# Two attention layers in one stream: units interleaved so that a slot's scores and maxima belong to one layer

## The chip, the cores and the metric

The kernel runs on one core of a Trainium2 chip. The metric is the device time of one execution in microseconds (us); lower is better. Three runs of the kernel before gave 1993.62, 1994.18 and 1994.74 us.

Engines are named as the profile does: PE is TensorE (PEld its weight loads), DVE is VectorE, ACT is ScalarE, POOL is GpSimd, SP is SyncE, which here only issues DMAs. PE writes to PSUM, of which this kernel has eight banks in use in the attention stage.

## The reference

Four layers run one after the other on a batch of 8, 256 channels by 512 positions, each added to its input. The change touches only how the first two are ordered against each other:

```python
# layer 0: 16 heads of 16; mask on the keys
Q, K, V = proj(Wq), proj(Wk), proj(Wv)
att = (Q @ K^T / sqrt(16) + b) * m + (1 - m) * NEG
x = x + softmax(att) @ V
# layer 1: 8 heads of 32, keys = queries = values; mask on both sides
qh = x^T @ Wq^T
logits = (qh @ qh^T / sqrt(32) * cmask + (1 - cmask) * NEG) * rmask
x = x + (softmax(logits) @ qh) @ Wo^T
# layer 2: a GRU over 256 steps; layer 3: block attention and layer norm
```

Layer 1 of a batch item needs layer 0 of the same item. Different items do not depend on each other, so layer 1 of one item can run beside layer 0 of the next. The GRU starts when all eight items are done.

## The kernel before

**Units and slots.** The work of one item is cut in six *units* of four heads each: units 0 to 3 are the groups of layer 0, units 4 and 5 those of layer 1 (`UNITS`). A unit has four *slots*, one for each block of 128 keys, so one turn of the loop has 24 slots. In a slot PE does four score matmuls (`ST<-Q,K`, 128 keys by 512 queries, one per head), and ACT takes the exponential of each into `pr`; then the products with the values (`AV<-pr,...`) of the slot before follow, for layer 1 also the sums of the exponentials (`DN<-pr,ones`).

**Maxima.** The softmax needs each query's maximum first. So every unit has, some slots earlier, four slots of *maxima*: PE computes the scores once more, the other way round (`MX<-K,Q`, 128 queries by 512 keys), and DVE reduces each (`mx<-MX`). After the fourth slot of maxima a small transposition (`maxT`, `MX<-identz,mx`) turns them into rows; ACT copies the negated row, POOL splits it in two numbers (`nmp`) and sends both by DMA into two extra rows of the stacked queries, so that the scores come out with the maximum taken off. The scores of a unit wait for this DMA (`nm_dma`).

**Which rows.** Layer 0's stacked operands have 51 (maxima) or 53 rows (scores), and heads lie in pairs at partitions 0 and 64: two such matmuls run side by side on the array. Layer 1's have 97 or 99 rows, and two matmuls run one after the other.

**The order.** A list `ORDER` fixes the order of all these steps, and each engine walks it in order (`Walk`), taking out what is its own. In a slot it is: two scores, two maxima, the value product of the slot before, two scores, two maxima, and then extra steps by a table: projections (`proj`), values, the turning back of a finished unit (`den`, `finish`), `back` and `out`. Maxima stand `LEAD` = 7 slots ahead of their scores. With that lead, slots 0 to 8 of a turn have scores and maxima of layer 0, slots 9 to 15 scores of layer 0 and maxima of layer 1, slot 16 both of layer 1, and slots 17 to 23 scores of layer 1 and maxima of layer 0. Layer 1 runs one item behind layer 0 (`OFF`). The first two turns have a rule of their own (`at_turn`), which takes some maxima eight slots earlier.

**Banks and buffers.** `MX` has three banks in turn, shared by maxima, transpositions and all projections; `ST` has three, so a score waits for the exponential three scores back (`exped`). `AV` and `DN` have one each. Stacked operands of each unit exist once: a unit's stack for the next item is loaded after its last score.

**Stacking.** A projection comes out of PE, ACT and DVE split it in `hi` and `lo`, SP writes both to DRAM (`d_piece`, `pieces`), and reads them back in the stacked layout (`stack`, six or twelve DMAs a unit). Layer 1's queries are masked by POOL in between (`hi_q`, `lo_q`). All this hangs on one SP queue, whose order is written out in the loop at its end. The first maximum of a unit waits for its stack (`stacked`).

Of the kernel before, what the change touches and what calls it, by code (L numbers as in the profile page):

```python
# [5 lines left out]
def attention_layers(nc, xT, K0, ident, to_clear, cleared, preload, preload_late, xt_in, x, mask, wq0, wk0, wv0, b0, wq1, wo1, ident_in):  # L6
# [19 lines left out]
    OFF = [0 if L == 0 else -1 for L, g in UNITS]  # L26
# [6 lines left out]
    with ExitStack() as ctx:  # L33
# [77 lines left out]
        LEAD = 7  # L111

        def at_slot(s):

            w, kc = divmod(s, KC)
            (u, qb, o), = [(u, qb, OFF[u] + (1 if KC * u - LEAD + qb < 0 else 0))
                           for u in range(NU) for qb in range(KC) if (KC * u - LEAD + qb) % SLOTS == s]
            top = [("max", (u, qb, i), o) for i in range(4)]
            pw, pk = divmod((s - 1) % SLOTS, KC)
# [3 lines left out]
            if qb == 0:  # L123

                before = (u - 1) % NU
                t = KC * before - LEAD + KC
                steps.append(("maxT", (before,), OFF[before] + (1 if t < 0 else 0)))
            steps += [st[2], st[3], top[2], top[3]]
            if kc == 1:
                before = (w - 1) % NU  # L130
                o = OFF[before] - (1 if w == 0 else 0)
                if UNITS[before][0] == 1:
                    steps.append(("den", (before,), o))
                steps.append(("finish", (before,), o))
            extra = {1: [("proj", ("q0", 0), 1)], 2: [("proj", ("k0", 0), 1)],
                     3: [("proj", ("q0", 1), 1)], 4: [("proj", ("k0", 1), 1)],
                     6: [("back", (1, 0), -2), ("back", (1, 1), -2)], 7: [("out", (0,), -2)], 8: [("out", (1,), -2)],
                     9: [("values", (1, 0), -1)], 10: [("values", (1, 1), -1)],
                     18: [("back", (0, 0), 0), ("back", (0, 1), 0)],
                     19: [("values", (0, 0), 1)], 20: [("proj", ("k1", 0), 0)], 21: [("proj", ("k1", 1), 0)],  # L140
                     22: [("values", (0, 1), 1)]}
            return steps + extra.get(s, [])

        def at_turn(it, s):
            steps = [(name, a, it + o) for name, a, o in at_slot(s)]
            if it in (0, 1):


                early = lambda step: step[0] in ("max", "maxT") and step[1][0] < 2 and step[2] == 1
                ahead, o = divmod(it * SLOTS + s + 8, SLOTS)  # L150
                own = [step for step in steps if not early(step) and there(step[2])]
                top, turn = ([step for step in ((name, a, ahead + of) for name, a, of in at_slot(o)) if early(step) and step[0] == kind]
                             for kind in ("max", "maxT"))
                steps = []
                for step in own:
                    steps.append(step)
                    if step[0] == "av":
                        steps, turn = steps + turn, []
                    elif step[0] == "score" and step[1][2] % 2 == 1:
                        n = 2 if step[1][2] == 1 else len(top)  # L160
                        steps, top = steps + top[:n], top[n:]
                steps += turn + top
            return steps
        ORDER = [step for it in range(-1, B + 2) for s in range(SLOTS) for step in at_turn(it, s) if there(step[2])]


# [63 lines left out]
        def _(sp):  # L230
# [76 lines left out]
            def first_layer(b):  # L307
                for m in range(2):
                    for side in ("q0", "k0"):
                        pieces(b, side, m)  # L310
# [3 lines left out]
            def second_layer(b, m):  # L314
                for side in ("k1", "q1"):
                    pieces(b, side, m)
                if m == 0:
                    load_in(b + 2)
# [1056 lines left out]
```

## Time and profile before

| | |
|---|---|
| median of three runs | 1994.18 us (1993.62 to 1994.74) |
| profiled execution, time | 1992.88 us |
| profiled execution, span | 1991.1 us |
| PE busy | 1853.8 us, 93% |
| DVE busy | 1144.0 us, 57% |
| ACT busy | 799.3 us, 40% |
| attention stage on PE | first maximum at 33.05 us, last matmul of `out` ends at 947.7 us |

The span is from the first to the last instruction; the time of the execution is 1.8 us longer. The stage that the change touches takes the first 948 us; the rest is the GRU and the last layer, whose instructions do not change. PE's busy time is the union of modelled matmul times, so a PE that looks busy can still be filled badly: what counts is the distance from the start of one slot to the start of the next. A slot starts here with the first of its score matmuls (line 557). Read this way, the five full turns in the middle repeat to within 0.1 us.

### The profile page before, as it was taken

What the parts mean: (1) busy time and instruction counts of PE and PEld (TensorE: products, weight loads), DVE (VectorE), ACT (ScalarE), POOL (GpSimd) and SP (SyncE); (2) the same over time, 40 slices, a digit from 0 to 9 for tenths busy, and PEclk for the clock granted to TensorE, in tenths of its full rate; (3) what the DMA queues carried; (4) which work ended last, traced back from release to release, by engine and by line L of the source; (5) the groups of instructions that cost most, each with busy time, mean ns of one, the idle gap of its engine ahead of it and who ended that gap; (6) DMA issues with size and microseconds to landing.
All of it is one profiled execution on the core that took longest, in us unless ns stands there. A gap on an engine that the chain in (4) does not pass through costs nothing. (4 is left out here: it accounts for less than half of the span.)

```text
span 1991.1 us, 85497 instructions
## 1 busy us (share of the span) xinstructions
PE 1853.8 (93%) x37678; PEld 1269.8 (64%) x37678; DVE 1144.0 (57%) x3363; ACT 799.3 (40%) x2195; POOL 391.5 (20%) x862
## 2 busy tenths in 40 slices
PE   5989999999999999988899999999999999999983
PEld 2434444444444344444899989988888888888861
DVE  4767575766666576723445555555555555555567
ACT  0556565656555565634222222222222222222234
POOL 0121212021211112110131222211222211222113
PEclk7899999999999999988999999999999999999995
DMA  5654433516152534040300000000000000000002
GB/s 146 227 138 141 118 114 87 154 45 185 46 170 65 164 82 124 2 149 1 114 13 13 13 12 13 5 13 13 13 12 11 6 13 12 13 13 10 7 3 85
DMA packets 65521, 127.65 MB, mean 64 GB/s; under 512 B 15545, under 2 KB 22201, under 8 KB 61556
## 3 DMA queue, kind: packets, MB, share of 16 engines
q1 hardware_dynamic: 62076, 121.35, 20.7%
q8 instruction: 296, 4.85, 1.0%
q0 software_dynamic: 3072, 0.82, 0.2%
q14 instruction: 77, 0.63, 0.1%
HBM read 77.56 MB, written 37.85 MB: 58 GB/s over the span
## 5 line engine op out<-in xcount | busy, mean ns | idle before, releaser
L416 DVE TENSOR_REDUCE mx<-MX 128x1 f32<-128x512 f32 x768 | 485.4, 683 | 200.0 <-PE MX L537 199.8
L964 PE MATMUL gate<-whh,state 128*8 128x128 f32 x16384 | 503.6, 273 | 34.0 <-DVE state L880 24.5
L964 PEld LDWEIGHTS gate<-whh,state 128*8 128x8 f32 x16384 | 428.6, 91 | 92.1 <-DVE state L880 86.4
L473 ACT ACTIVATE pr<-ST 128x512 f32<-128x512 f32 x768 | 412.0, 601 | 165.9 <-PE ST L557 165.6
L964 PE MATMUL pg<-whh,state 128*8 128x128 f32 x8192 | 277.1, 273 | 0.3 <-issue 0.3
L857 DVE STREAM_TRANSPOSE trn<-gate 128x128 f32<-128x128 f32 x256 | 81.2, 317 | 337.2 <-PE gate L964 337.2
L912 ACT ACTIVATE rg<-pre 128x32 f32<-128x32 f32 x256 | 58.8, 230 | 505.4 <-DVE pre L859 505.4
L537 PE MATMUL MX<-K,Q 51*128 51x512 f32 (+1 forms) x768 | 246.4, 469 | 14.1 <-DMA Q<-d_rows 9.4
L557 PE MATMUL ST<-Q,K 53*128 53x512 f32 (+1 forms) x768 | 241.0, 486 | 10.5 <-ACT pr L473 10.4
L557 PEld LDWEIGHTS ST<-Q,K 53*128 53x128 f32 (+1 forms) x768 | 99.0, 187 | 207.6 <-ACT pr L473 117.8
L964 PEld LDWEIGHTS pg<-whh,state 128*8 128x8 f32 x8192 | 229.2, 90 | 0.9 <-issue 0.7
L816 POOL TENSOR_TENSOR xT<-xT,state 128x32 f32<-128x32 f32 x256 | 66.9, 261 | 736.3 <-DVE state L880 736.3
L938 PE MATMUL pg<-xT,wih 128*32 128x128 f32 x4096 | 183.0, 275 | 11.5 <-issue 8.7
L537 PEld LDWEIGHTS MX<-K,Q 51*128 51x128 f32 (+1 forms) x768 | 110.0, 194 | 104.1 <-issue 45.1
L361 POOL TENSOR_TENSOR nmp<-nm,zero 16x128 fp32r<-16x128 f32 x48 | 21.5, 447 | 621.5 <-ACT nm L489 621.5
L573 PE MATMUL AV<-pr,va 128*17 128x512 f32 x1024 | 135.6, 601 | 0.9 <-ACT pr L473 0.9
L914 ACT ACTIVATE state<-pre 128x64 f32<-128x64 f32 x256 | 66.7, 261 | 164.6 <-DVE pre L868 164.6
L938 PEld LDWEIGHTS pg<-xT,wih 128*32 128x32 f32 x4096 | 116.0, 110 | 26.2 <-issue 24.8
L880 DVE TENSOR_TENSOR_SCAN state<-by,state 128x48 f32<-128x48 f32 x512 | 104.3, 245 | 41.4 <-ACT by L917 41.4
L948 PE MATMUL gate<-wihZ,xT 128*32 128x128 f32 x2048 | 112.8, 273 | 1.8 <-PEq L33 1.4
L917 ACT ACTIVATE by<-trn 128x16 f32<-128x16 f32 x512 | 90.9, 225 | 22.9 <-DVE trn L871 0.7
L862 DVE STREAM_TRANSPOSE trn<-gate 128x128 f32<-128x128 f32 x256 | 80.9, 316 | 25.2 <-PE gate L964 1.2
(185 smaller groups left out, 1893.5 us busy)
## 6 DMA issues: line engine op xcount, KB each, us to landing
d_q<-hi_q SPq DMA_DIRECT2D x32, 256.0 KB, 3.2
d_q<-lo_q SPq DMA_DIRECT2D x32, 256.0 KB, 3.9
d_k<-hi_k SPq DMA_DIRECT2D x32, 256.0 KB, 3.8
d_k<-lo_k SPq DMA_DIRECT2D x32, 256.0 KB, 3.9
K<-d_k SPq DMA_DIRECT2D x64, 128.0 KB
Q<-d_q SPq DMA_DIRECT2D x64, 128.0 KB
K<-d_k SPq DMA_DIRECT2D x16, 512.0 KB
Q<-d_q SPq DMA_DIRECT2D x16, 512.0 KB
```

The source lines that it names most:

```text
L416: dve.reduce_max(mx[:, u, col:col + 1], bank[:, :], AX.X).then_inc(mx_red, 1)
L473: act.activation(pr[:, kc % 2, i], ST[n % 3][:, :], ACT.Exp, scale=SCALE[UNITS[w][0]]).then_inc(exped, 1)
L537: pe.matmul(bank[:, :], Q[r, h, tok(qb)], K[r, h, :], start=True, stop=True).then_inc(mx_mm, 1)
L557: pe.matmul(ST[n % 3][:, :], K[r, h, tok(kc)], Q[r, h, :], start=True, stop=True).then_inc(st_mm, 1)
L573: last = pe.matmul(AV[r, :], v, pr[:, kc % 2, i, :], start=kc == 0, stop=kc == KC - 1)
L857: dve.transpose(trn[:, R, :], psR[:, 0:P]).then_inc(s_tr, 1)
L862: dve.transpose(trn[:, N, :], psN[:, 0:P]).then_inc(s_tr, 1)
L880: dve.tensor_tensor_scan(state[:, 1 - q, W3 * a:W3 * a + W3], by[:, half(a)].rearrange("p c b v -> p (c b v)"), threes(q, a), 0.0, ALU.mul ...
L917: a.activation(by[:, half(z), :, 2], tr[Z][:, half(z)], ACT.Sigmoid).then_inc(s_z[z], 1)
L938: last = pe.matmul(gb[i % 2][32 * j:32 * j + 32, 0:TG * B], wih[:, n, i * P + 32 * j:i * P + 32 * j + 32], xT[:, n, TG * blk:TG * (blk + 1 ...
L948: last = pe.matmul(zb[32 * j:32 * j + 32, P * w:P * (w + 1)], xT[:, k, t0:t0 + 4, :].rearrange("p t b -> p (t b)"), wihZ[:, k, P * w:P * ( ...
L964: last = pe.matmul(bank[32 * j:32 * j + B, lo:hi], held[q][:, c, :], whh[:, c, o + lo:o + hi], start=first, stop=done)
```

## The change

The order of the six units in a turn becomes a list, `PLACES` = (0, 1, 5, 2, 3, 4): scores go through the units in this order, four slots each. Maxima are taken for the unit three places later: beside scores of 0, 1, 5, 2, 3, 4 stand maxima of 2, 3, 4, 0, 1, 5. Unit 5 now runs two items behind layer 0, unit 4 one. The extra steps move to other slots, `at_turn` loses its rule for the first turns, and the loop has one turn more at its end. SP's order follows. No instruction of PE, ACT, DVE or POOL is added or removed, and the same DMAs are issued.

```diff
-    OFF = [0 if L == 0 else -1 for L, g in UNITS]
+    OFF = [0 if L == 0 else -1 - g for L, g in UNITS]
...
-        LEAD = 7
+        PLACES = (0, 1, 5, 2, 3, 4)
+        LEAD = len(PLACES) // 2
...
-            w, kc = divmod(s, KC)
-            (u, qb, o), = [(u, qb, OFF[u] + (1 if KC * u - LEAD + qb < 0 else 0))
-                           for u in range(NU) for qb in range(KC) if (KC * u - LEAD + qb) % SLOTS == s]
+            p, kc = divmod(s, KC)
+            w = PLACES[p]
+
+            def maxima(p):
+                u = PLACES[(p + LEAD) % NU]
+                return u, OFF[u] + (1 if p + LEAD >= NU else 0)
...
-            extra = {1: [("proj", ("q0", 0), 1)], 2: [("proj", ("k0", 0), 1)],
...
-                     19: [("values", (0, 0), 1)], 20: [("proj", ("k1", 0), 0)], 21: [("proj", ("k1", 1), 0)],
...
+            extra = {0: [("proj", ("k1", 0), -1)], 2: [("proj", ("q0", 0), 1)], 3: [("proj", ("k0", 0), 1)],
+                     4: [("proj", ("k1", 1), -1)], 5: [("proj", ("q0", 1), 1)], 7: [("proj", ("k0", 1), 1)],
+                     14: [("back", (1, 0), -2), ("back", (1, 1), -2)], 15: [("out", (0,), -2)], 16: [("out", (1,), -2)],
+                     17: [("values", (1, 0), -1)], 18: [("values", (1, 1), -1)],
+                     21: [("values", (0, 0), 1)], 22: [("back", (0, 0), 0), ("back", (0, 1), 0)], 23: [("values", (0, 1), 1)]}
...
-        ORDER = [step for it in range(-1, B + 2) for s in range(SLOTS) for step in at_turn(it, s) if there(step[2])]
+        ORDER = [step for it in range(-1, B + 3) for s in range(SLOTS) for step in at_turn(it, s) if there(step[2])]
...
-            for it in range(-1, B):
+            for it in range(-1, B + 1):
+                layer(it - 1, ("k1", "q1"), 0)
+                place(it - 1, LAST0 + 1)
+                layer(it + 1, ("q0", "k0"), 0)
+                place(it + 1, 0)
+                layer(it - 1, ("k1", "q1"), 1)
...
+                place(it + 1, 1)
+                place(it - 1, LAST1)
+                place(it + 1, 2)
+                place(it + 1, LAST0)
+                load_in(it + 2)
```

Three places on PE show it. In the rows `ST` and `MX` are PSUM banks of scores and maxima, `K0,Q0` are the stacks of layer 0, `K1,Q1` those of layer 1. Line numbers of the change are 17 lower.

**In a full turn**, a slot with scores of layer 1. Before, PE had:

```order
L557 MATMUL ST1<-Q1,K1 128x512
L557 MATMUL ST2<-Q1,K1 128x512
L537 MATMUL MX2<-K0,Q0 128x512
L537 MATMUL MX0<-K0,Q0 128x512
L573 MATMUL AV<-pr,vb 32x512 x4
L576 MATMUL DN<-pr,ones 32x512 x4
L557 MATMUL ST0<-Q1,K1 128x512
L557 MATMUL ST1<-Q1,K1 128x512
L537 MATMUL MX1<-K0,Q0 128x512
L537 MATMUL MX2<-K0,Q0 128x512
```

Now such a slot reads:

```order
L540 MATMUL ST0<-Q1,K1 128x512
L540 MATMUL ST1<-Q1,K1 128x512
L520 MATMUL MX2<-K1,Q1 128x512
L520 MATMUL MX0<-K1,Q1 128x512
L556 MATMUL AV<-pr,vb 32x512 x4
L559 MATMUL DN<-pr,ones 32x512 x4
L540 MATMUL ST2<-Q1,K1 128x512
L540 MATMUL ST0<-Q1,K1 128x512
L520 MATMUL MX1<-K1,Q1 128x512
L520 MATMUL MX2<-K1,Q1 128x512
```

The scores and the products are the same; the maxima between them were of layer 0 and are of layer 1. The maxima of layer 0 now stand only in slots whose scores are of layer 0.

**At the end of the attention stage**, where the last item's layer 1 begins. Before, PE had, after the last value products of item 6, its turning back and its output projection, and then the first maxima of item 7:

```order
L573 MATMUL AV<-pr,vb 32x512 x4
L576 MATMUL DN<-pr,ones 32x512 x4
L557 MATMUL ST0<-Q1,K1 128x512
L557 MATMUL ST1<-Q1,K1 128x512
L573 MATMUL AV<-pr,vb 32x512 x4
L576 MATMUL DN<-pr,ones 32x512 x4
L583 MATMUL MX1<-sel,rawd 128x4 x4
L591 MATMUL MX2<-identz,raw 128x128 x4
L630 MATMUL MX0<-identz,yT1 128x128 x4
L630 MATMUL MX1<-identz,yT1 128x128 x4
L638 MATMUL MX2<-w1,ctxs 128x256 x4
L638 MATMUL MX0<-w1,ctxs 128x256 x4
```

Now the two projections of item 7 (`w1`) come directly ahead of the scores and maxima that use them:

```order
L556 MATMUL AV<-pr,vb 32x512 x4
L559 MATMUL DN<-pr,ones 32x512 x4
L527 MATMUL MX2<-identz,mx 16x128
L587 MATMUL MX0<-x1,w1 128x512 x2
L566 MATMUL MX1<-sel,rawd 128x4 x4
L574 MATMUL MX2<-identz,raw 128x128 x4
L587 MATMUL MX0<-x1,w1 128x512 x2
L540 MATMUL ST1<-Q1,K1 128x512
L540 MATMUL ST2<-Q1,K1 128x512
L520 MATMUL MX1<-K1,Q1 128x512
L520 MATMUL MX2<-K1,Q1 128x512
L540 MATMUL ST0<-Q1,K1 128x512
```

Of these, the two rows on `K1,Q1` into `ST` are scores of item 6, and the rows into `MX` at the end are the first maxima of item 7, unit 4, for which the first projection in this piece is needed. The turning back and output of item 6 moved behind them.

**Ahead of the last unit's scores.** Before, the transposition of the last unit's maxima is followed by the scores of unit 4 and their products:

```order
L544 MATMUL MX0<-identz,mx 16x128
L557 MATMUL ST2<-Q1,K1 128x512
L557 MATMUL ST0<-Q1,K1 128x512
L557 MATMUL ST1<-Q1,K1 128x512
L557 MATMUL ST2<-Q1,K1 128x512
L573 MATMUL AV<-pr,vb 32x512 x4
L576 MATMUL DN<-pr,ones 32x512 x4
L557 MATMUL ST0<-Q1,K1 128x512
L557 MATMUL ST1<-Q1,K1 128x512
L557 MATMUL ST2<-Q1,K1 128x512
L557 MATMUL ST0<-Q1,K1 128x512
L573 MATMUL AV<-pr,vb 32x512 x4
```

Now it stands after all scores of unit 4, and the last unit's scores follow it after one turning back (`sel`, `raw`):

```order
L556 MATMUL AV<-pr,vb 32x512 x4
L559 MATMUL DN<-pr,ones 32x512 x4
L527 MATMUL MX0<-identz,mx 16x128
L566 MATMUL MX1<-sel,rawd 128x4 x4
L574 MATMUL MX2<-identz,raw 128x128 x4
L540 MATMUL ST0<-Q1,K1 128x512
L540 MATMUL ST1<-Q1,K1 128x512
L540 MATMUL ST2<-Q1,K1 128x512
```

The distance between the last maxima and the scores that need them shrank to the two steps between.

## Rows read from the trace of the kernel before

**Rows 1.** Stretches: us, busy of PE, PEld, DVE, ACT, POOL, PEclk, DMA share, GB/s.

```profile
449.49:559.23 109.74, 107.06 (x591) 47.40 (x588) 71.81 (x118) 63.16 (x123) 19.66 (x29) 1.00 0.39 112
449.49:490.95 41.46, 39.27 (x214) 16.73 (x211) 28.98 (x47) 25.54 (x50) 3.96 (x8) 1.00 0.66 187
```

**Rows 2.** Timeline, scores and maxima of layer 0, no extra step (start us, us).

```profile
792.22 0.51 PE L557 MATMUL ST<-Q,K 53*128 53x512 f32 x2
...
792.76 2.06 ACT L473 ACTIVATE pr<-ST 128x512 f32<-128x512 f32 x4 [0.86 <-PE ST L557]
...
795.14 0.50 PE L557 MATMUL ST<-Q,K 53*128 53x512 f32 x2
```

**Rows 3.** Timeline, PE: the same kind of slot, just after one with an extra step.

```profile
152.94 0.49 PE L557 MATMUL ST<-Q,K 53*128 53x512 f32 x2
...
155.22 0.40 PE L557 MATMUL ST<-Q,K 53*128 53x512 f32 x1
```

**Rows 4.** Timeline, PE: scores of layer 0, maxima of layer 1.

```profile
392.40 0.49 PE L557 MATMUL ST<-Q,K 53*128 53x512 f32 x2
...
395.64 0.50 PE L557 MATMUL ST<-Q,K 53*128 53x512 f32 x2
```

**Rows 5.** Timeline, PE: scores of layer 1, maxima of layer 0.

```profile
335.73 0.82 PE L557 MATMUL ST<-Q,K 99*128 99x512 f32 x2
...
336.92 1.07 PE L573 MATMUL AV<-pr,vb 128*32 128x512 f32 x8
337.80 1.04 PE L576 MATMUL DN<-pr,ones 128*32 128x512 f32 x8
...
339.77 0.69 PE L557 MATMUL ST<-Q,K 53*128 53x512 f32 x2
```

**Rows 6.** Timeline, PE: scores and maxima of layer 1, value products of layer 0.

```profile
297.44 0.68 PE L557 MATMUL ST<-Q,K 99*128 99x512 f32 x2
...
300.61 0.40 PE L557 MATMUL ST<-Q,K 99*128 99x512 f32 x1
```

**Rows 7.** Timeline, PE: from slot to slot over a projection, layer 0's, then layer 1's.

```profile
465.21 0.51 PE L557 MATMUL ST<-Q,K 53*128 53x512 f32 x2
...
469.85 0.50 PE L557 MATMUL ST<-Q,K 53*128 53x512 f32 x2
...
536.19 0.82 PE L557 MATMUL ST<-Q,K 99*128 99x512 f32 x2
...
541.75 1.03 PE L557 MATMUL ST<-Q,K 99*128 99x512 f32 x2
```

**Rows 8.** Timeline, PE: scores of layer 1 with no maxima beside them.

```profile
916.02 0.96 PE L557 MATMUL ST<-Q,K 99*128 99x512 f32 x3
...
919.55 0.96 PE L557 MATMUL ST<-Q,K 99*128 99x512 f32 x3
```

**Rows 9.** Timeline, DVE: maxima with no scores beside them.

```profile
33.88 7.26 DVE L416 TENSOR_REDUCE mx<-MX 128x1 f32<-128x512 f32 x12 [8.86 <-PE MX L537]
```

**Rows 10.** Timeline, last item: layer 1's first projection, unit 4's stack, unit 5's.

```profile
856.08 1.88 PE L604 MATMUL MX<-x,w 128*128 128x512 f32 x4
...
865.96 1.14 SPq L286 DMA_DIRECT2D K<-d_k  x2
...
878.49 1.14 SPq L286 DMA_DIRECT2D K<-d_k  x2
```

**Rows 11.** Timeline, the last unit's row of maxima: transposition, DMA.

```profile
912.18 0.38 PE L544 MATMUL MX<-identz,mx 128*16 128x128 f32 x2
...
913.88 1.00 POOL L372 DMA_DIRECT2D Q<-nmp  x2
```

**Rows 12.** The page, DMA issues: KB each, median us to landing.

```profile
Q<-nmp POOLq DMA_DIRECT2D x96, 8.0 KB, 2.1
```

**Rows 13.** Timeline, PE: the output projection of item 6, and of item 7.

```profile
879.81 6.71 PE L638 MATMUL MX<-w,ctxs 128*128 128x256 f32 x16 [0.68 <-ACT ctxs L515]
...
943.99 3.72 PE L638 MATMUL MX<-w,ctxs 128*128 128x256 f32 x16 [0.73 <-ACT ctxs L515]
```

More of the change, by code:

```diff
@@ L109, in half_of @@
             return w // 2 if w <= LAST0 else w - LAST0 - 1
-        LEAD = 7
+        PLACES = (0, 1, 5, 2, 3, 4)
+        LEAD = len(PLACES) // 2
         def at_slot(s):
-            w, kc = divmod(s, KC)
-            (u, qb, o), = [(u, qb, OFF[u] + (1 if KC * u - LEAD + qb < 0 else 0))
-                           for u in range(NU) for qb in range(KC) if (KC * u - LEAD + qb) % SLOTS == s]
-            top = [("max", (u, qb, i), o) for i in range(4)]
-            pw, pk = divmod((s - 1) % SLOTS, KC)
+            p, kc = divmod(s, KC)
[3 more added lines that the diff above has]
+                return u, OFF[u] + (1 if p + LEAD >= NU else 0)
+            u, o = maxima(p)
+            top = [("max", (u, kc, i), o) for i in range(4)]
+            earlier = (s - 1) % SLOTS
+            pw, pk = PLACES[earlier // KC], earlier % KC
             st = [("score", (w, kc, i), OFF[w]) for i in range(4)]
             steps = [st[0], st[1], top[0], top[1], ("av", (pw, pk), OFF[pw] - (1 if s == 0 else 0))]
[L123 to L127, printed above, removed]
+            if kc == 0:
+                u, o = maxima((p - 1) % NU)
+                steps.append(("maxT", (u,), o - (1 if p == 0 else 0)))
             steps += [st[2], st[3], top[2], top[3]]
             if kc == 1:
-                before = (w - 1) % NU
-                o = OFF[before] - (1 if w == 0 else 0)
+                before = PLACES[p - 1]
+                o = OFF[before] - (1 if p == 0 else 0)
                 if UNITS[before][0] == 1:
@@ L142, in at_slot @@
             return steps + extra.get(s, [])
         def at_turn(it, s):
[L145 to L162, printed above, removed]
@@ L163, in at_turn @@
-            return steps
-        ORDER = [step for it in range(-1, B + 2) for s in range(SLOTS) for step in at_turn(it, s) if there(step[2])]
+            return [(name, a, it + o) for name, a, o in at_slot(s)]
+        ORDER = [step for it in range(-1, B + 3) for s in range(SLOTS) for step in at_turn(it, s) if there(step[2])]
         number = {}
@@ L305, in stack, with layer, place @@
                     put(Q1[3 * n:3 * n + 1, of, :], d_rows[b:b + 1, 4:5, :].to_broadcast([1, 4, T]))
-            def first_layer(b):
-                for m in range(2):
-                    for side in ("q0", "k0"):
+            def layer(b, sides, m):
+                if there(b):
+                    for side in sides:
                         pieces(b, side, m)
-                    for w in units_of(0, m):
-                        stack(b, w)
[L314 to L318, printed above, removed]
-                for w in units_of(1, m):
-                    stack(b, w)
-            for it in range(-1, B):
+            def place(b, w):
+                if there(b):
+                    stack(b, w)
+            for it in range(-1, B + 1):
[4 more added lines that the diff above has]
+                layer(it - 1, ("k1", "q1"), 1)
                 if there(it):
```

15 lines of the change are left out of this document (2 added, 13 removed).

## The prediction, made before the changed kernel ran

> **What bounds the kernel now.** I read the page first: the span and PE's share (93%). Then busy time by stretch: in a full turn of 109.74 us PE is busy 107.06, DVE 71.81, ACT 63.16, and DMA is a share of 0.39 [rows 1]. So in the middle of the attention stage PE bounds, and what a turn costs is the sum of its slots' lengths on PE. I then read the timeline of PE, from the first score matmul of a slot to that of the next, for each kind of slot. The reader is to see that the kinds differ although the matmuls are alike:
>
> - Both of layer 0: 2.92 us, with ACT idle 0.86 us before its four exponentials, which take 2.06 [rows 2]. Here PE is not the bound: the second pair of scores waits for its banks. After a slot with an extra step the same work takes 2.28 us [rows 3]. PE's own need is thus about 2.28, and 0.65 is a wait that other work can fill.
> - Scores of layer 0, maxima of layer 1: 3.24 [rows 4]; over several such slots 3.2.
> - Scores of layer 1, maxima of layer 0, with `DN`: 4.04 [rows 5]. `DN` is 0.88 of it: the `AV` products start at 336.92 and `DN` at 337.80, for the same work.
> - Both of layer 1: seen only beside `AV` of layer 0, 3.17 [rows 6]. With `DN` I take 3.17 + 0.88 = 4.05. This is the main kind that the trace doesn't show. From above it is bounded by the mixed slot's 4.04, if sorting is worth nothing; from below by 3.9, if half of the 0.24 to 0.3 us between two pairs of unlike shape goes. I keep 4.05, the sum of rows, as the value, and 3.9 as the low end.
>
> Last I read the end of the stage, for what the last item waits for.
>
> **The steady part, counted.** The order gives how many slots of each kind there are in all. Before: 78 with both of layer 0, 49 mixed with scores of layer 0, 42 mixed with scores of layer 1, 8 with both of layer 1 and no `DN`, 14 with scores of layer 1 alone, 1 with scores of layer 0 alone, 15 with maxima alone. Now: 120, 0, 0, 15, 4, 8, 12, and 45 with both of layer 1 and `DN`. Scores of layer 1 alone take 3.53 [rows 8]; of layer 0 alone no row shows; ACT's 2.06 is the lower bound, 2.92 with maxima the upper, and 3.53 less `DN`, 2.65, is what I take. Maxima alone are 7.26 us for 12, so 2.42 for four [rows 9].
>
> For both of layer 0 the bounds are 2.28 and 2.92. The nine such slots at the start of a turn last 41.46 us [rows 1]; their extra steps I put at 16.7 (four projections 7.6, two output products 3.8 by rows 13, one `DN` 0.9, and by estimate 4.4 for turning back and `maxT`). That leaves 2.75 each, and I take that.
>
> Before: 78 x 2.75 + 49 x 3.2 + 42 x 4.04 + 8 x 3.17 + 14 x 3.53 + 2.65 + 15 x 2.42 = 654.8. Now: 120 x 2.75 + 15 x 3.17 + 45 x 4.05 + 4 x 3.53 + 8 x 2.65 + 12 x 2.42 = 624.2. The difference is **-30.6 us**; with 2.92 it is -23.5, with 2.28 it is -50.3. All of it comes from slots of layer 0: a mixed pair costs 7.24, a sorted one 6.80.
>
> **What the moved steps give back.** Layer 1's projections stood in slots with scores of layer 1 and cost 541.75 - 536.19 - 4.04 = 1.52 each; in slots of layer 0 a projection costs 4.64 - 2.75 = 1.89 [rows 7], because a bank of `MX` is then held until ACT and DVE have both read it. 16 x 0.37 = +5.9. `DN` of a unit's last slot falls into a slot of layer 0 twelve times instead of six: 6 x 0.88 = +5.3. Layer 1's values, now in slots of layer 0: +1. Together **+12**. `back` and `values` of layer 0 stay in slots of layer 1: nothing. The SP queue: each stack now has eight slots (over 30 us) between its last reader and its first maximum, where it had thirteen. From the start of a layer 1 projection to the end of its stack I find 18 us (below), so nothing waits in a full turn; POOL's rows have eight slots where they had three.
>
> A rule that speaks for more than this: the Trainium skill, TensorEngine Tiling (Array Packing), section Key Properties, says that changing the tiling mode drains TensorE. A mixed pair has ten such changes, a sorted pair four. The rows bear it out only where PE is the bound: (7.24 - 2.28 - 4.05) / 6 = 0.15 us a change. By the rule the gain of the slots would be -50.3, not -30.6; it is the first rival.
>
> **The ends.** Here the change loses, since layer 1 of the last item is spread over more of the order.
>
> - *Waiting for the last stack.* Before, layer 1's first projection for the last item starts at 856.08, its stack's first DMA is issued at 865.96, and the second unit's stack, which waits for pieces queued behind the first stack, at 878.49 [rows 10]. The first stack is then in place between 869.5 (all issued) and 878; I take 874.5, 18.4 us after the projection's start. Before, PE had the scores of unit 5 and the whole turning back and output of item 6 to do meanwhile. Now, by the order, after this projection come only `den`, `finish`, the second projection and two scores, 6 us. **+12.5 us** (8 to 16).
> - *After it* PE restarts at half clock. What this costs can be seen on the output products: 6.71 us for item 6, after waits of PE, and 3.72 for item 7 [rows 13]. +3 for the first slots after the wait, and -3 because item 6's output now follows busy work: 0.
> - *Three more ends of a run of scores,* where the products wait for the last exponential, less one that goes: +2.4.
> - *The last row.* From the transposition to the end of POOL's issue are 2.70 us [rows 11], to landing some 2 more [rows 12]. Before, fourteen score matmuls stood between; now `den` and `finish`, about 2 us. +2.8.
> - *The start:* four more maxima before the first score and none of the eight-slots-early rule, +1.5. In the second turn four slots have maxima of layer 1 alone, at the risk of half clock after: +1.5 (0 to 3).
>
> Together **+20.7**.
>
> **The sum.** -30.6 + 12.2 + 20.7 = +2.3 us. Walking through the new order stretch by stretch instead, with the same slot lengths, I get +1.6 up to the second turn, -9 over that turn, 5 x -2.3 over the full turns, +3 in the turn that has no new item, and +24 from there to the end: +8. The two differ in how much of the waits the extra steps fill. I take the middle, **+5**: the profiled execution of 1992.88 would be 1998, and on the median of 1994.18, which lies 1.3 above it, **1999 us**. A full turn should be 107.4 us, 2.3 less, and the attention stage end near 953.
>
> **Rivals.**
>
> 1. *The drains are what costs, everywhere.* Extra steps fill all waits in slots of layer 0, which come down to 2.28, halfway 2.5. For it: rows 3. Against it: the nine slots of [rows 1] have extra steps in seven and still average 2.75. Full turn 104 to 106; time by the sum -50.3 + 12.2 + 20.7 = -17, halfway -8: 1977 to 1987, say **1986**. This is the one that ends on the other side, faster; it decides if the average of slots of layer 0 falls below 2.6.
> 2. *Slots of layer 0 get longer, not shorter.* Sixteen in place of nine, six projections in them in place of four, three banks of `MX` for all: the average stays at 2.92 and each extra step costs in full. For it: DVE idles in projection slots while the bank waits for ACT. -23.5 + 12.2 + 25 = +14: **2008**.
> 3. *The end costs nothing.* The last stack arrives early, since x1 and the other stacks are not in its way: the wait is 5 instead of 12.5, with the sum as it is otherwise: **1992**, no change.
> 4. That the change doesn't do what it says: the order shows that it does. A deadlock or a late stack in the full turns would need 30 us of DMA where 18 are seen; less than 1 in 50.
>
> **Chances.** The forecast 0.55 (own range 1992 to 2005), rival 1 0.23, rival 2 0.12, rival 3 0.10. The range that leaves out 2 in 10 is 1983 to 2009. A difference of 0.2% is 4 us, about what a measurement tells from none. Faster by more: 0.23 of rival 1 and a little of the others, 0.27. Within: rival 3 and the lower third of the forecast's range, 0.31. Slower: 0.42.
>
> **What would show it.** In the changed profile: slots with both of layer 1 at 4.05 and 3.17; slots of layer 0 at 2.75 on average over a turn; a full turn from one xin load to the next at 107.4; a wait of PE of some 12 us for a stack, near the end, ended by a DMA into `K1` or `Q1`, with half clock after it. The forecast is wrong if a full turn is under 106 or over 109, or if that wait is under 8 or over 17 us.

## The result: faster by 0.47%

| | before | changed |
|---|---|---|
| median of 9 runs each, same chip | 1994.74 us (1990.89 to 2005.3) | 1985.56 us (1975.8 to 1994.08) |
| profiled execution, time and span | 1992.88, 1991.1 us | 1987.19, 1985.4 us |
| first matmul of the GRU | 949.1 us | 945.6 us |

The ratio is 0.9953, with a 95% interval of 0.9935 to 0.9971. 1999 us was forecast; rival 1 had said 1986. The changed kernel was run once more beside before (e8 below), with 0.9962 (0.9946 to 0.9977).

The attention stage of both, by stretch: to the second turn, the second turn, five full turns, the rest up to the GRU. Columns as in [rows 1]. Before:

```profile
0.00:127.16 127.16, 100.08 (x396) 43.83 (x396) 74.58 (x128) 46.34 (x88) 19.62 (x37) 0.84 0.54 162
127.16:230.04 102.88, 99.30 (x531) 42.07 (x531) 64.92 (x108) 60.48 (x117) 20.78 (x28) 1.00 0.47 132
230.04:778.65 548.61, 535.23 (x2942) 236.93 (x2940) 359.20 (x590) 315.76 (x611) 98.27 (x145) 1.00 0.40 115
778.65:949.10 170.45, 155.92 (x840) 75.68 (x837) 79.95 (x130) 83.67 (x163) 21.42 (x33) 0.91 0.20 60
```

The changed kernel:

```profile
0.00:123.72 123.72, 94.47 (x389) 41.00 (x390) 73.42 (x126) 44.21 (x86) 17.53 (x35) 0.85 0.60 164
123.72:223.26 99.54, 97.02 (x444) 41.06 (x444) 67.17 (x112) 50.48 (x99) 18.03 (x26) 0.85 0.44 123
223.26:751.02 527.76, 512.71 (x2941) 235.03 (x2940) 358.53 (x590) 310.43 (x610) 99.20 (x145) 1.00 0.42 116
751.02:945.64 194.62, 166.95 (x935) 80.99 (x935) 78.49 (x128) 92.82 (x182) 26.35 (x38) 0.91 0.23 71
```

-3.4, -3.3, -20.9 and +24.2 make -3.5 us. The rest of the span's 5.7 is a GRU and last layer whose instructions did not change: their part is 1041.9 us before, 1039.8 after. Over the fourteen profiles of this study this part took between 1037.1 and 1043.3 us with the same instructions, so 2 us there say nothing on the order. Of the 9.2 us between the medians the profiles thus show 3.5 as the attention stage's own (3.7 in the second pair, e8 and e11). Both profiled executions of the changed kernel were slower than their medians (1987.19 against 1985.56, 1988.34 against 1983.84); where the rest of the 9.2 comes from is not shown.

A full turn here is one pass of the loop with work of every kind in it. Within one, PE is busy 102.52 of 105.53 us, where it was 107.06 of 109.74 [rows 1]:

```profile
434.27:539.80 105.53, 102.52 (x589) 47.00 (x589) 71.70 (x118) 62.09 (x122) 19.85 (x29) 1.00 0.42 116
```

The timeline of PE in that turn, a plain slot of layer 0 behind a projection, which answers to [rows 3]; it lasts 2.23 us:

```profile
463.67 0.50 PE L540 MATMUL ST<-Q,K 53*128 53x512 f32 x2
464.01 0.40 PE L520 MATMUL MX<-K,Q 51*128 51x512 f32 x2
464.33 1.05 PE L556 MATMUL AV<-pr,va 128*17 128x512 f32 x8
465.32 0.49 PE L540 MATMUL ST<-Q,K 53*128 53x512 f32 x2
465.65 0.75 PE L520 MATMUL MX<-K,Q 51*128 51x512 f32 x2
465.90 1.09 PE L540 MATMUL ST<-Q,K 53*128 53x512 f32 x2
```

A slot of layer 0 with one half of an output, 4.24 us (499.46 to 503.70), and PE waits for nothing in it:

```profile
499.46 0.50 PE L540 MATMUL ST<-Q,K 53*128 53x512 f32 x2
...
501.77 1.99 PE L621 MATMUL MX<-w,ctxs 128*128 128x256 f32 x8
503.70 0.50 PE L540 MATMUL ST<-Q,K 53*128 53x512 f32 x2
```

And the new kind, both of layer 1 with `DN`, which no row of before could show: 4.27 us, from 478.64 to 482.91; its neighbour takes 4.12.

```profile
478.64 0.70 PE L540 MATMUL ST<-Q,K 99*128 99x512 f32 x2
479.18 0.91 PE L520 MATMUL MX<-K,Q 97*128 97x512 f32 x2
480.02 1.06 PE L556 MATMUL AV<-pr,vb 128*32 128x512 f32 x8
480.90 1.04 PE L559 MATMUL DN<-pr,ones 128*32 128x512 f32 x8
481.88 0.73 PE L540 MATMUL ST<-Q,K 99*128 99x512 f32 x2
482.44 0.63 PE L520 MATMUL MX<-K,Q 97*128 97x512 f32 x2
482.91 0.40 PE L540 MATMUL ST<-Q,K 99*128 99x512 f32 x1
```

In the second turn, where four slots have maxima of layer 1 alone, the clock falls to 1.2 GHz at about 164 us and comes back near 195:

```profile
160.00:170.00 10.00, 9.38 (x26) 4.32 (x25) 9.72 (x18) 0.97 (x2) 1.94 (x4) 0.71 0.89 208
170.00:180.00 10.00, 10.00 (x37) 3.88 (x37) 5.72 (x10) 4.57 (x11) 1.89 (x4) 0.50 0.36 97
180.00:190.00 10.00, 10.00 (x37) 3.48 (x34) 5.13 (x9) 5.37 (x12) 0.77 (x2) 0.50 0.32 79
190.00:200.00 10.00, 9.96 (x55) 4.86 (x54) 6.78 (x12) 5.54 (x12) 1.26 (x3) 0.76 0.05 8
```

DVE is busy 9.72 of the first ten us and takes one maximum at a time. PE waits for it, and then runs the next slots of layer 0 at half the clock while busy throughout. Near the end stand the three waits the prediction spoke of, in the timeline of PE; the first one is for the last item's stack, the second for the last row of maxima, and the third row is the last output, now partly at half clock [rows 10, 11, 13]:

```profile
848.28 1.04 PE L540 MATMUL ST<-Q,K 99*128 99x512 f32 x2
861.33 1.22 PE L520 MATMUL MX<-K,Q 97*128 97x512 f32 x2 [12.01 <-DMA Q<-d_rows]
...
912.63 0.63 PE L574 MATMUL MX<-identz,raw 128*128 128x128 f32 x4
915.02 3.25 PE L540 MATMUL ST<-Q,K 99*128 99x512 f32 x6 [1.76 <-DMA Q<-nmp]
...
938.70 5.51 PE L621 MATMUL MX<-w,ctxs 128*128 128x256 f32 x16 [0.67 <-ACT ctxs L498]
```

### The profile page after: what moved, and what is told of

Its sections match the earlier page's. It is cut to its first block and busy times, and to the rows that moved or that the text cites. A ratio compares the mean times of both kernels' runs of the same rounds, so it can differ in the third digit from the quotient of the medians.

```text
span 1985.4 us, 85497 instructions
## 1 busy us (share of the span) xinstructions
PE 1830.9 (92%) x37678; PEld 1268.2 (64%) x37678; DVE 1143.2 (58%) x3363; ACT 789.8 (40%) x2195; POOL 392.4 (20%) x862
## 5 line engine op out<-in xcount | busy, mean ns | idle before, releaser
L520 PE MATMUL MX<-K,Q 51*128 51x512 f32 (+1 forms) x768 | 238.7, 444 | 25.3 <-DMA Q<-d_rows 22.5
L921 PE MATMUL pg<-xT,wih 128*32 128x128 f32 x4096 | 173.6, 274 | 7.7 <-issue 6.7
L520 PEld LDWEIGHTS MX<-K,Q 51*128 51x128 f32 (+1 forms) x768 | 121.6, 196 | 78.5 <-DVE mx L399 38.8
L931 PE MATMUL gate<-wihZ,xT 128*32 128x128 f32 x2048 | 108.0, 273 | 1.4 <-PEq L33 1.4
```

The source lines that it names most:

```text
L520: pe.matmul(bank[:, :], Q[r, h, tok(qb)], K[r, h, :], start=True, stop=True).then_inc(mx_mm, 1)
L921: last = pe.matmul(gb[i % 2][32 * j:32 * j + 32, 0:TG * B], wih[:, n, i * P + 32 * j:i * P + 32 * j + 32], xT[:, n, TG * blk:TG * (blk + 1 ...
L931: last = pe.matmul(zb[32 * j:32 * j + 32, P * w:P * (w + 1)], xT[:, k, t0:t0 + 4, :].rearrange("p t b -> p (t b)"), wihZ[:, k, P * w:P * ( ...
```

## The experiments

All but e4 and e11 are timed against before on their own chip; ratios carry 95% intervals.

**e1: the places kept, the sorting undone.** With maxima two places ahead instead of three, sixteen of the 24 slots are mixed again.

```diff
-        LEAD = len(PLACES) // 2
+        LEAD = 2
```

> The change with maxima two places ahead instead of three, and nothing else altered: scores still go 0, 1, 5, 2, 3, 4 and every extra step keeps its slot, but per turn 8 slots have both of layer 0, 8 mix scores of layer 0 with maxima of layer 1, and 8 mix scores of layer 1 with maxima of layer 0; none has both of layer 1. Theory A (sorting the shapes on PE is the gain): a sorted pair costs 2.62 + 4.05 = 6.7 us, a mixed pair 7.2, so a full turn goes from 105.6 to about 109.7, and the whole is 25 to 30 us slower than the change, slower than the kernel before. Theory B (the gain comes from where the extra steps stand, which fill waits in slots of layer 0): a full turn stays within 1 us of 105.6, and the time within 5 us of the change.

Measured: ratio 1.0301 (1.0276 to 1.0325), 2049.36 us against 1990.43. The full turn:

```profile
467.55:577.72 110.17, 108.58 (x590) 47.62 (x590) 72.08 (x118) 62.41 (x122) 19.81 (x29) 1.00 0.39 111
```

That is 4.6 us more than the changed kernel's, and 0.4 more than before's. Slot by slot the eight left sorted repeat to 0.02 us, the eight with scores of layer 0 and maxima of layer 1 add 3.6 us (0.45 each on average, 0.07 to 0.83 in single slots), the eight the other way round 1.06 (0.13 each). A mixed pair (one slot of each kind) thus costs 0.58 us more than a sorted one; the prediction had 0.44. Before has seven mixed pairs a turn and e1 eight, so of the 0.43 us between them the eighth pair is 0.58, and all the moved steps together are about -0.15. At 0.58 a pair, sorting is 4.1 of the 4.2 us that a turn gained, and moving the steps cost nothing. This takes the average of e1's pairs for those of before, which stand beside other steps.

Theory A gave 25 to 30 us for the whole and was far too low: e1's GRU starts 58.5 us later than the changed kernel's. 23 of these are the five full turns. The other 35 come from its ends: 24 before the second turn (148.08 us instead of 123.72), where only eight slots of the first turn have scores and maxima side by side, instead of sixteen, and 11 behind the last full turn.

**e4: what a change of shape costs by itself.** Between attention and GRU PE runs six sequences of matmuls that wait for nothing: *small* ones (51 rows, in pairs), *large* ones (97 rows) and *cols* (the eight rows of an `AV` of one slot).

```diff
+            for n in range(12):
+                small(0), small(1), small(0), small(1), large(0), large(1), large(0), large(1)
...
+            for n in range(24):
+                small(0), small(1), large(0), large(1)
...
+            for n in range(48):
+                small(0), small(1)
...
+            for n in range(48):
+                large(0), large(1)
...
+            for n in range(12):
+                cols()
+                small(0), small(1), small(0), small(1)
...
+            for n in range(12):
+                cols()
+                large(0), large(1), large(0), large(1)
```

> The change with extra matmuls on PE between the attention stage and the GRU, which nothing reads and which wait for nothing but each other: pairs of 51 rows (two side by side) and pairs of 97 rows, in runs of like pairs, in alternation, and each beside column-tiled value products. The whole is longer by their length. Theory A (a change of shape on the array costs PE time of its own): pairs in alternation take longer than the mean of two runs of like pairs, by 0.15 us for each change of shape. Theory B (no such cost; mixed slots are longer for waits on ACT and DVE): alternation costs less than 0.03 us a change.

The six stretches, in the order of the diff (one profile, not timed):

```profile
943.52:965.01 21.49, 21.48 (x97) 11.68 (x97) 0.00 (x0) 0.00 (x0) 0.00 (x0) 1.00 0.00 1
965.99:992.09 26.10, 26.10 (x100) 11.61 (x97) 0.00 (x0) 0.00 (x0) 0.00 (x0) 1.00 0.00 1
993.07:1004.20 11.13, 11.13 (x100) 8.95 (x97) 0.00 (x0) 0.00 (x0) 0.00 (x0) 1.00 0.01 1
1005.18:1027.17 21.99, 21.99 (x101) 17.96 (x97) 0.00 (x0) 0.00 (x0) 0.00 (x0) 1.00 0.00 0
1029.01:1048.76 19.75, 19.75 (x148) 5.16 (x144) 0.00 (x0) 0.00 (x0) 0.00 (x0) 1.00 0.01 2
1048.76:1070.96 22.20, 22.20 (x129) 8.73 (x125) 0.00 (x0) 0.00 (x0) 0.00 (x0) 1.00 0.00 0
```

A stretch runs from the first start of its kind to the start of the next sequence, so each holds one change at its end. 96 small matmuls then take 11.13 - 0.2 = 10.93 us, 0.114 each, and 96 large ones 21.79, 0.227 each. The first sequence has 48 of each, 16.36 us, and 24 changes: (21.49 - 16.36) / 24 = 0.21 a change. The second has the same matmuls and 48 changes: 9.74 / 48 = 0.20. One `cols` is 0.86 us (two in a row before a small one last 1.84, one 0.98). The fifth stretch has twelve groups of four small ones, twelve `cols` and 24 changes: (19.75 - 15.78) / 24 = 0.17; the sixth eleven groups of large ones, ten `cols` and 21 changes: (22.20 - 18.59) / 21 = 0.17. A change thus has a price of its own, the same after two matmuls as after four. The Trainium skill, TensorEngine Tiling (Array Packing), Key Properties, says that changing the tiling mode drains TensorE, with no figure; the trace agrees that a change takes time, 0.17 to 0.21 us, though it can't show that the time is a drain.

With these numbers half of e1 can be accounted for. A mixed slot has three more changes than a sorted one: 0.60 us. Scores of layer 1 with small maxima instead of large: 0.60 - 4 x 0.113 = +0.15, measured +0.13. Scores of layer 0 with large maxima: 0.60 + 0.45 = +1.05, measured +0.45. Part of the missing 0.60 is waits that the sorted slot still has and the mixed one fills: over these eight slots PE idles 1.97 us in a full turn of the changed kernel (0.72 for exponentials, the rest for maxima on DVE and for ACT's copy of them) and 0.43 in e1, 0.19 a slot. The other 0.4 a slot stays open.

**e5: the extra steps bunched.** Turning back and both output halves stand in slot 14, both values steps in slot 17; slots 15, 16 and 18 lose theirs.

```diff
-                     14: [("back", (1, 0), -2), ("back", (1, 1), -2)], 15: [("out", (0,), -2)], 16: [("out", (1,), -2)],
-                     17: [("values", (1, 0), -1)], 18: [("values", (1, 1), -1)],
+                     14: [("back", (1, 0), -2), ("back", (1, 1), -2), ("out", (0,), -2), ("out", (1,), -2)],
+                     17: [("values", (1, 0), -1), ("values", (1, 1), -1)],
```

> The change as it is, but the steps that stand alone in the layer 0 slots 14, 15, 16 (turning back, output, output) stand together in slot 14, and both values steps in slot 17: slots 15, 16 and 18 lose their step. Nothing else moves. Theory A (an extra step costs less than its own time, since it fills the wait for the exponentials of its slot): slots 15, 16 and 18 rise by 0.4 to 0.65 us over what they have less their step, slot 14 takes the two output halves at their full 1.9 us each, and a full turn goes from 105.55 to 106.8 to 107.5; five full turns +6 to +10. Theory B (a step costs its own time wherever it stands; slots of layer 0 are short in the changed kernel for another reason): a full turn stays within 0.3 us of 105.55.

Measured: ratio 1.0033 (1.0011 to 1.0054). The full turn, the same work:

```profile
429.48:536.66 107.18, 102.75 (x589) 47.44 (x588) 71.45 (x118) 61.97 (x122) 19.86 (x29) 1.00 0.42 114
```

107.2 against 105.5: the same steps cost 1.65 us more a turn in two heaps, so theory B is out, and the total is theory A's. Its slots are not. Set against their length in the changed kernel without their step, slots 15 and 18 are 0.1 us shorter and slot 16 is 0.2 longer, where 0.4 to 0.65 was expected of all three. The wait for exponentials is back only one slot behind the first plain one: 0.22 and 0.25 us in slots 16 and 17, and slot 19 is 0.54 longer. The other part is in the two heaps, each 0.56 us longer than its slot and its steps were apart. In slot 14 it is the output, which now waits for ACT's copy of what was turned back, a wait that another slot's work covered in the changed kernel:

```profile
494.09 0.63 PE L613 MATMUL MX<-identz,yT 128*128 128x128 f32 x4 [0.28 <-DVE mx L399]
495.39 3.72 PE L621 MATMUL MX<-w,ctxs 128*128 128x256 f32 x16 [0.67 <-ACT ctxs L498]
```

So spread steps do cost less than bunched ones, for two kinds of wait: that for exponentials, and that of one step for the step ahead of it.

**e2: a new order at the end.** The scores of item 6's unit 5 stand between the projections of item 7 and its first maxima, where before had them; turning back and output of item 6 lie beside the maxima.

```diff
+        for k in range(KC):
+            ORDER += end_slot(score=(5, k, six), av=(5, k - 1, six) if k else None)
+        ORDER += end_slot(av=(5, 3, six), extra=[("den", (5,), six), ("finish", (5,), six)])
+        ORDER += [("back", (1, 0), six), ("back", (1, 1), six)]
+        ORDER += end_slot(top=(4, 0, seven))
+        ORDER += end_slot(top=(4, 1, seven), extra=[("out", (0,), six)])
...
```

> The change with the order after the last turn rewritten: the scores of unit 5 of item 6 come before the wait for the last item's stack, without maxima between them; den, finish and back of item 6 too; out and values stand among the maxima of unit 4 of item 7, and two slots of maxima of unit 5 stand ahead of the scores of unit 4. Theory A (the end's wait of 12.0 us for the stack, the cold slots behind it and the wait for the last row are a cost of the new order that another order avoids): the attention stage ends 12 to 14 us earlier than with the change, at about 931 us, and the time falls as much, to about 1973. Theory B (the wait is only moved, since the work put into it was hiding the reduction of the maxima): it ends less than 4 us earlier.

Measured: 0.9945 (0.9924 to 0.9966), 1978.17 us against 1990.43; the GRU starts at 937.1 us, 8.5 earlier. Theory A had 12 to 14 us and a start at 931, theory B less than 4: neither. The wait of 12.01 us is gone, so it did cost; not all of it came back. From the start of item 7's turn the stage takes 187.3 us instead of 194.6, so 7.4 are the new end's and 1.2 come from a shorter head. Part of what is missing is half clock in the work behind. PE in its timeline, with the waits just before and at the fall of the clock, at 865.6 us (0.78 granted over 860 to 870 us):

```profile
860.91 1.06 PE L585 MATMUL AV<-pr,vb 128*32 128x512 f32 x8 [0.94 <-ACT pr L485]
...
864.02 1.05 PE L595 MATMUL MX<-sel,rawd 128*128 128x4 f32 x8 [1.19 <-ACT rawd L495]
...
866.42 1.97 PE L642 MATMUL MX<-identz,yT 128*128 128x128 f32 x8 [0.85 <-DVE yT L452]
```

**e7: the same with maxima begun earlier,** beside the last scores of item 6, and unit 5's beside scores of unit 4.

```diff
-            ORDER += end_slot(score=(5, k, six), av=(5, k - 1, six) if k else None)
+            ORDER += end_slot(score=(5, k, six), top=(4, 0, seven) if k == 3 else None, av=(5, k - 1, six) if k else None)
...
+        ORDER += end_slot(score=(4, 0, seven), top=(5, 1, seven))
+        ORDER += end_slot(score=(4, 1, seven), top=(5, 2, seven), av=(4, 0, seven))
+        ORDER += end_slot(score=(4, 2, seven), top=(5, 3, seven), av=(4, 1, seven))
```

> The tail order again, with the first maxima of item 7's unit 4 started beside the last scores of item 6's unit 5 and all maxima of unit 5 but the first four beside scores of unit 4. Theory A (what is left at the end is that maxima and scores stand apart, 1.9 us a pair of slots, and the half clock from 865 to 897 us after the gaps around turning back): the GRU starts 4 to 8 us earlier than in the tail order (937.1), at 929 to 933. Theory B (the last item's chain of DMAs, transposition and exponentials sets the end, whatever PE does meanwhile): 935 to 938.

Measured: 0.9922 (0.9899 to 0.9945), GRU at 932.0, inside theory A's 929 to 933. But 1.8 of the 5.1 us lie ahead of item 7's turn: from the start of item 7's turn to the GRU it takes 184.0 us, in e2 187.3, in the changed kernel 194.6. The end itself is 3.3 shorter, where theory A had 4 to 8.

**e3: the second turn's lone maxima moved** beside the scores of slots 12 to 15.

```diff
+                if 12 <= s <= 15:
+                    at = [n for n, step in enumerate(steps) if step[0] == "max" and step[1][2] in (1, 3)]
+                    for n, half in zip(reversed(at), ((2, 3), (0, 1))):
+                        steps[n + 1:n + 1] = [("max", (LAST0 + 1, s - 12, i), 0) for i in half]
```

> The change with the four slots of the second turn that hold only maxima (unit 4, item 0) dissolved: these maxima stand beside the scores of unit 2 in the next four slots, where layer 0's maxima already are. Theory A (that run of maxima alone lets the granted clock of PE fall, and the nine slots behind it run at 4.6 to 5.0 us instead of 2.9): the clock stays at 1.00 from 157 to 200 us; the four slots take 5.0 to 5.3 us by DVE, and the third turn starts 6 to 10 us earlier than at 223.3 us. Theory B (the clock falls all the same, since DVE is the bound in the doubled slots): it starts less than 3 us earlier, or later.

Measured: 0.9997 (0.9979 to 1.0015), third turn at 222.22 us instead of 223.26. Theory B, and a miss for the repair: eight maxima a slot keep DVE the bound, the clock falls at the same place, and slots 13 to 15 take 7.3 us each.

**e6: the same maxima spread thinner,** two behind each of slots 7 and 12 to 18.

```diff
+                if s in (7, *range(12, 19)):
+                    n = 0 if s == 7 else s - 11
+                    steps += [("max", (LAST0 + 1, n // 2, 2 * (n % 2) + i), 0) for i in range(2)]
```

> The change, but in the second turn the sixteen maxima of unit 4, item 0, that stood alone in slots 8 to 11 are spread two a slot behind slots 7 and 12 to 18. Theory A (PE falls to half clock because it waits for DVE in a stretch of maxima; with six maxima a slot DVE needs 6 x 0.6 = 3.6 us and PE some 2.8): the granted clock stays 1.00 from 157 to 200 us and the third turn starts at 214 to 219 instead of 223.3. Theory B (the fall at 165 us has nothing to do with the maxima that stand alone, as the run in which they were moved beside slots 12 to 15 hints: it fell at the same time): half clock again from 165 to some 190, third turn at 222 to 226.

Measured: 0.9956 (0.9938 to 0.9973), third turn at 218.0. The clock still falls at 162 us, but is back at 173. Neither theory as stated; in e9, with the same second turn, the third began at 221.3. So this order doesn't settle the cause.

**e10: the lone maxima computed twice.** Sixteen matmuls more, nothing moved.

```diff
+                if b == 0 and u == LAST0 + 1:
+                    pe.matmul(bank[:, :], Q[r, h, tok(qb)], K[r, h, :], start=True, stop=True)
                 pe.matmul(bank[:, :], Q[r, h, tok(qb)], K[r, h, :], start=True, stop=True).then_inc(mx_mm, 1)
```

> The change, with each of the sixteen maxima matmuls of unit 4, item 0, issued twice into the same bank: 3.7 us more work for PE in slots 8 to 11 of the second turn, where it waits for DVE otherwise (2.4 us a slot). Theory A (half clock comes from PE's waits for DVE in these slots): the fall at 165 us is gone or short, slots 13 to 17 are back at 2.9, 2.9, 2.9, 3.1 and 4.3, third turn at 214 to 217. Theory B (half clock comes from something else): it falls at the same place, and the third turn starts at 223 or up to 4 us later.

Measured: 0.9946 (0.993 to 0.9962), 1977.91 us against 1988.79. Its third turn starts at 216.68, 6.6 us earlier than in the changed kernel's first profile, with more work on PE:

```profile
160.00:170.00 10.00, 10.00 (x46) 5.24 (x38) 9.69 (x18) 0.83 (x3) 2.01 (x4) 1.00 0.90 213
170.00:180.00 10.00, 9.53 (x44) 3.54 (x43) 7.77 (x13) 6.78 (x14) 1.89 (x4) 0.83 0.51 124
180.00:190.00 10.00, 9.27 (x62) 4.40 (x62) 8.17 (x15) 6.72 (x15) 2.04 (x4) 1.00 0.33 85
190.00:200.00 10.00, 9.98 (x62) 4.63 (x58) 7.25 (x12) 8.04 (x17) 1.06 (x3) 1.00 0.24 64
```

DVE is as busy as in the changed kernel in the first stretch and sets the pace, but PE has no gaps and keeps 2.4 GHz there; only 3.4 us near 173 are at half. One profile would not do, since the spell changes from execution to execution. Six profiles (the changed kernel twice, e2, e4, e5, e7) have the same instructions up to slot 13 of the second turn: in them the spell lasts 10.2 to 30.7 us and the turn takes 92.6 to 99.5. In the two profiles with doubled maxima (this one and e12) it lasts 3.4 us and not at all, and the turn takes 92.0 and 90.7. The shortest of the six is e5's:

```profile
160.00:170.00 10.00, 9.44 (x26) 4.61 (x25) 9.28 (x18) 1.83 (x5) 1.54 (x5) 0.64 0.94 208
170.00:180.00 10.00, 9.57 (x50) 3.18 (x48) 7.54 (x13) 6.10 (x13) 1.04 (x3) 0.84 0.23 66
```

So filling PE's short waits for DVE keeps the clock up for most or all of the stretch, and theory A holds for the clock; how much time that gives lies between 0.6 and 8.8 us by which profiles are compared. The timed ratios do not tell e10 (0.9946) from the change (0.9953 and 0.9962). The Trainium skill, TensorE: Matmul & The Clock Gate, A second HAM failure mode: psum-queue depth-cycling, tells of a kernel in which short idle times between groups of matmuls, as PSUM banks go round, let the clock go up and down; the trace agrees, with PE busy 9.38 of 10 us where the clock falls in the changed kernel and 10.00 of 10 here.

**e9 and e12: parts together.** e9 has e6's spread maxima and e7's end with two repairs: the first maxima one slot later, and `den` and `finish` of unit 4 ahead of the last unit's scores. e12 has e10's doubled maxima and e9's end.

```diff
+        ORDER += end_slot(top=(4, 0, seven))
...
+        ORDER += end_slot(av=(4, 3, seven), extra=[("den", (4,), seven), ("finish", (4,), seven)])
+        ORDER += end_slot(score=(5, 0, seven))
```

> Both repairs in one kernel: the spread maxima of unit 4 in the second turn, and the new order at the end, there with the first maxima of item 7 one slot later (after the scores of item 6's last unit) and with den and finish of unit 4 put between the last row's transposition and the scores that need it. Theory A (the parts add): the third turn starts some 4 to 5 us earlier than in the changed kernel, the end is another 13 to 16 us shorter than there (13.7 with the first new order; the two waits of 2.53 and 2.86 us mostly go), so the GRU starts at 924 to 930, against 945.7, and the median is 1964 to 1972. Theory B (the waits at the end move to other places and the cold start stays): GRU start 931 to 937, median 1973 to 1980.

> The doubled maxima of the run before, in place of the spread ones, together with the new order at the end of the run that had both. Theory A (the second turn's half clock and the end are separate costs and add): third turn at 213 to 216, GRU start at 923 to 928, median 9 to 14 us under that of the run with spread maxima and the new end when both are set against before: a ratio of 0.988 to 0.992. Theory B (a shorter start makes the end colder or its transfers later, as between the tail orders): GRU start 929 to 932 and a ratio of 0.993 to 0.995.

Measured for e9: 0.9945 (0.9931 to 0.9958), GRU at 930.6. The two waits that it was to remove went, from 2.53 to 0.27 us and from 2.86 to none, and from the start of item 7's turn to the GRU it is 181.6 us; but its third turn starts only 2 us earlier than the changed kernel's, and the median and GRU start are theory B's (1973 to 1980, 931), not theory A's 1964 to 1972. For e12: **0.9882 (0.9867 to 0.9896), 1965.4 us against 1987.63.** Its third turn starts at 215.88 us and its GRU at 926.5:

```profile
926.55 3.70 PE L960 MATMUL gate<-wihZ,xT 128*32 128x128 f32 x128 [1.44 <-PEq L33]
```

Theory A held: the two repairs add. e9 and e12 differ only in how they treat the second turn's maxima, spread or doubled, and their ratios (0.9945 and 0.9882) lie clear of each other. This is the best kernel of the study, 22 us under before where the change alone brings 9.

**e8 and e11: both kernels once more.**

> The changed kernel once more, unchanged, beside the kernel before on the same chip. If the 8.6 us between the medians is the change's: a ratio of 0.994 to 0.998, attention end 943 to 947 in its profile, full turns 105.5. If part of it was the spread of the unchanged GRU stage: a ratio nearer 1, with the attention stage some 3 to 6 us shorter than 949.1 as in the first profile.

> The kernel before, unchanged, for a second profile. If the attention stage of before repeats from execution to execution (no half clock after 65 us but at the last item): GRU start within 1 us of 949.1, full turns 109.7. If it has spells of its own: a difference of several us, which would put part of the measured gain down to chance.

e8: 0.9962 (0.9946 to 0.9977), full turns of 105.6 us, GRU at 945.7. e11, one profile: full turns of 109.7, GRU at 949.4, 0.3 from the first. So before's attention stage repeats, and the gain is the change's, though the profiles show less of it (3.5 and 3.7 us) than the medians (9.2 and 8.9).

## Why the prediction was wrong

- **What failed is the steady part, in two terms.** A full turn was to be 107.4 us and is 105.5. The sorted pair was set at 0.44 us less than a mixed one (7.24 and 6.80); it is 0.58 less (e1), 1.0 us over a turn's seven pairs. And the moved steps were set at **+12** in all, 5.9 of it because a projection costs "1.89" in a slot of layer 0 and 5.3 for `DN` in such slots; by e1 they cost about nothing (-0.15 a turn), the other 0.9 us of the turn.
- **In slots, it is the "2.75" for a slot of layer 0.** The eight slots of layer 1 in a full turn sum to 37.6 us, so the sixteen of layer 0 are 67.9. With each step's own time on PE taken off (25.8 us in all) that is 2.64 a slot. The nine slots of before, reckoned alike, have 2.78. The sixteen are not fuller: eleven have a step from the table, where before seven of nine had. But the steps are of other kinds. The eight slots with the projections keep 2.69, the eight with turning back, output and values 2.58. The new kind, both of layer 1 with `DN`, erred the other way: 4.12 and 4.27 for the 4.05 that was set, and the low end of 3.9 did not come.
- **Why the steps cost less is shown in part.** Slots 1 to 7 take 30.4 us with four projections and 23.5 in the turn that has none of these four: 1.74 each, not 1.89. In the kernel before the same four, in slots 1 to 4, cost 2.00 each (25.07 us against 17.06 over slots 1 to 5). e5 shows that spreading other steps is worth 1.65 us a turn. Which of these waits made up the whole 0.9 us was not taken apart.
- **Rival 1 is nearest to what came.** It had a turn of 104 to 106 and 1986 us; 105.5 and 1985.6 were measured. But it was to decide "if the average of slots of layer 0 falls below 2.6", and 2.64 is just over. Its strong form, 2.28 and all of the drains, did not come: a pair's six changes are worth 1.2 us (e4), of which half is seen. "0.15 us a change" was right in kind and low: alone it is 0.17 to 0.21. That its 1986 was met within 0.5 us is luck in part: the start and the second turn missed by 5 us and more in opposite directions, and the profiles show only 3.5 to 3.7 us of the medians' 9 in the attention stage.
- **By stretch,** forecast and measured: start +1.6 and -3.4; second turn -9 and -3.3; full turns -11.5 and -20.9; the turn with no new item +3 and -2.4; from there to the end +24 and +26.5. The full turns and the turn after them miss by 14.8 us together, the start by 5.0, the other way go the second turn with 5.7 and the end with 2.5. At the start 3.4 us is a shift: before, item 0's two projections of layer 1, 1.72 us each, stand ahead of the second turn, and now they stand in it.
- **The second turn** was mis-sized the other way: the "risk of half clock, +1.5 (0 to 3)". Slots 12 to 17 of that turn take 28.0 us; at full clock (slots 12 to 16 of the first turn, 17 of a full one) they are 17.9. In e10, where the half clock is nearly gone, they are 20.3 us, so most of the 10 was the clock's.
- **The ends were about right, +26.5 for +24:** a wait of 12.01 us for the stack, forecast 12.5; the last row 1.76, forecast 2.8; item 7's output at half clock, 5.51 instead of 3.72, not forecast. The two ways of summing stood 6 us apart (+2.3, +8) and I took the middle. Both shared the mis-sized terms, so neither could warn of the other.

## What to carry to other kernels

Price a slot's wait as something that other work can fill, and take an average over slots to other slots only where the kinds of step in them stay the same. Changes between matmul shapes are worth sorting out where PE is the bound, and less where it waits anyway: here about half of their price alone came back. When an order that repeats is re-sorted, look at its first and last turns on their own; here their repair was worth 19 us of attention stage (945.7 to 926.5), more than the change itself.

## What was not expected of the hardware

- More matmuls did not make the kernel slower: with 16 that compute nothing new, 3.6 us of PE work, the second turn took 92.0 and 90.7 us (e10, e12), and 92.6 to 99.5 without them, as the half clock in it went from 10.2 to 30.7 us down to 3.4 and none.
- The spell at 1.2 GHz in the second turn begins within a few us of the same place (162.9 to 165.8 us) but lasts differently from one execution to another, with the same instructions ahead of it: over 160 to 200 us the granted clock is 0.71, 0.50, 0.50, 0.76 in the changed kernel's first profile, and in e5, which differs only in the steps behind slot 14, it is back to full by 173.1, before slot 14 begins. e5's profile of 1987.49 us is the fastest of its ten runs, whose median is 1999.66. Part of the spread of the changed kernel's runs (1975.8 to 1994.08) may be this; it was not shown.
- A change between two matmul shapes costs 0.17 to 0.21 us, after two matmuls as after four (e4).
